# A transformer chain on one Trainium2 core: shared probability sums in the sequence attention, and three reorderings before it

## Time and profile before

| what | value |
|---|---|
| median of three runs | 1550.69 us (1550.03 to 1552.88) |
| profiled execution, its own time | 1555.64 us |
| its span, first to last instruction | 1553.9 us |
| busy share of the span | PE 90%, DVE 52%, ACT 47%, POOL 31% |
| granted TensorE clock, mean | 0.955 of full speed |

### The profile page before, as it was taken

One profiled execution on the slowest core, in us unless ns is written; L12 is line 12 of the kernel. 1 busy time (PEld: TensorE's weight loads), 2 busy tenths in 40 slices (PEclk: granted clock), 3 DMA queues, 4 the chain that ended last, 5 costly groups with the idle time before them and its releaser, 6 DMA issues. The chain is left out here.

```text
span 1553.9 us, 22502 instructions
## 1 busy us (share of the span) xinstructions
PE 1392.8 (90%) x8434; PEld 668.3 (43%) x8434; DVE 807.5 (52%) x1312; ACT 728.9 (47%) x1364; POOL 483.9 (31%) x522
## 2 busy tenths in 40 slices
PE   5678888788877989997899999989999999999998
PEld 4355655555533545552222222234444444444443
DVE  8864675566655778756666666525513211321220
ACT  3266666666665777772555565553501211210210
POOL 7211110356667676773222322144600000000000
PEclk9689999989989999997899999999999999999999
DMA  6646564746442001112644444233502002001000
GB/s 174 142 154 159 128 160 143 176 96 157 125 130 82 28 28 35 49 64 87 182 126 124 123 138 113 85 100 104 162 1 82 1 1 81 0 0 54 0 1 27
DMA packets 89447, 140.68 MB, mean 91 GB/s; under 512 B 8409, under 2 KB 47897, under 8 KB 88801
## 3 DMA queue, kind: packets, MB, share of 16 engines
q1 hardware_dynamic: 76544, 114.16, 27.0%
q10 hardware_dynamic: 12800, 25.17, 5.1%
HBM read 105.85 MB, written 33.46 MB: 90 GB/s over the span
## 5 line engine op out<-in xcount | busy, mean ns | idle before, releaser
L1792 DVE TENSOR_REDUCE c_negmax<-c_psA 128x1 f32<-128x512 f32 x256 | 165.9, 682 | 93.2 <-PE c_psA L1867 89.0
L2078 ACT ACTIVATE d_silu<-d_psGU 128x512 f32<-128x512 f32 x64 | 38.2, 596 | 344.7 <-PE d_psGU L2145 344.6
L2145 PE MATMUL d_psGU<-d_zt_hi,d_w_hi 128*128 128x512 bf16 x512 | 194.6, 380 | 4.0 <-ACT d_silu L2078 2.6
L2145 PE MATMUL d_psGU<-d_zt_lo,d_w_hi 128*128 128x512 bf16 x512 | 194.8, 381 | 0.0
L2145 PE MATMUL d_psGU<-d_zt_hi,d_w_lo 128*128 128x512 bf16 x512 | 194.8, 380 | 0.0
L1747 ACT ACTIVATE c_probs<-c_psB 128x512 f32<-128x512 f32 x256 | 140.4, 595 | 103.3 <-PE c_psB L1880 103.3
L894 DVE TENSOR_REDUCE a_negmax<-a_psX 128x4 f32<-128x1024 f32 x128 | 151.4, 1216 | 27.1 <-PE a_psX L1163 26.6
L2108 DVE TENSOR_TENSOR d_h<-d_psGU,d_silu 128x512 f32<-128x512 f32 x64 | 44.2, 691 | 223.7 <-PE d_psGU L2145 223.3
L753 ACT ACTIVATE a_probs<-a_psB 128x512 f32<-128x512 f32 x256 | 138.0, 592 | 18.8 <-PE a_psB L1175 18.2
L1867 PE MATMUL c_psA<-c_ks,c_qs 96*128 96x512 bf16 x256 | 104.0, 409 | 17.7 <-DVE c_negmax L1792 8.3
L1175 PE MATMUL a_psB<-a_qs,a_ks 115*128 115x256 bf16 x512 | 88.6, 292 | 33.4 <-ACT a_probs L753 31.4
(11 more groups left out here) (231 smaller groups left out, 2560.7 us busy)
## 6 DMA issues: line engine op xcount, KB each, us to landing
a_tern_stage<-in_w ACTq DMA_DIRECT2D x32, 768.0 KB, 5.8
d_weight_stage<-in_w_last SPq DMA_DIRECT2D x24, 512.0 KB, 4.2
a_ks<-k_scr SPq DMA_DIRECT2D x8, 768.0 KB
a_qs<-q_scr SPq DMA_DIRECT2D x8, 768.0 KB
c_ks<-k_scr SPq DMA_DIRECT2D x48, 128.0 KB, 2.6
c_qs<-q_scr SPq DMA_DIRECT2D x48, 128.0 KB, 3.0
a_xz<-in_x SPq DMA_DIRECT2D x32, 128.0 KB, 3.0
a_ctx<-in_ctx_t SPq DMA_DIRECT2D x8, 512.0 KB, 4.8
```

Of the source, the lines that this page charges most:

```text
L1792: v.tensor_reduce(negm[:, u:u + 1], A[:, u % 2, :], AX.X, ALU.max, negate=True)\
L2145: last = pe.matmul(GU[:, 2 * up + i % 2, :], wgu[wh][:, i, up, k, :], zt[zh][:, k, :], start=(k == 0 and j == 0), stop=(k == DC - 1 and j ...
```

## The change

In the masked attention all thirds of a group now come before `results`, and so does the normalisation of batch b+3 (at g == 6); the split of thirds over groups is new; the two logarithms of the weight scale come before the thirds; in the last batch the preparation of the FFN's first four tiles is dealt out in 12 parts over six groups.

In the ternary FFN `update(t - 3)` goes ahead of `gate(t, 1)` on DVE, one `take` moves up, and PE transposes x for tile t+1 ahead of `down(t - 2, 0)`.

In the sequence attention the exponentials have four buffers. For each quad, DVE adds key tile 0 and 1 of each head and POOL adds tile 2 and 3 (`added`, 128x512 f32 from SBUF to SBUF, four instructions each), and PE's `sums` then runs on each of the two added tiles: two groups of four matmuls for a quad in place of four. DVE's adds stand one by one between the maxima; the last quad keeps single sums for tiles 2 and 3. The end of a quad is spread over more time: `results` one step later, `turn_sums` at step 2 of the next quad, `turn_recips` and `finish` at the start of the quad after that.

```
-    THIRDS = (0, 2, 4, 1, 2, 1, 2, 0)
+    THIRDS = (0, 3, 3, 2, 1, 2, 1, 0)
...
-                    if g > 1:
-                        for k in behind[:1]:
-                            third(*k)
                     if to < BATCH:
                         exponentials(to, e + 1)
...
+                    for k in behind:
+                        third(*k)
+                    if g == 6 and b + 3 < BATCH:
+                        normalise(b + 3)
                     results(b, g)
...
-                    for k in behind[1 if g > 1 else 0:]:
-                        third(*k)
...
+                if t >= 3:
+                    update(t - 3)
                 if now:
                     gate(t, 1)
-                if t >= 3:
-                    update(t - 3)
...
-                    down(t - 3, n + 2) if n < 2 else down(t - 2, n - 2)
                     if n == 2:
                         for j in range(2):
                             transposed("x", t + 1, j)
+                    down(t - 3, n + 2) if n < 2 else down(t - 2, n - 2)
...
-        pr = sb("c_probs", [P, 2, 4, D], F32)
+        pr = sb("c_probs", [P, 4, 4, D], F32)
+        pairs = sb("c_prob_pairs", [P, 2, 4, D], F32)
...
+        def added(engine, unit, quads, pair, done, heads):
+            engine.wait_ge(s["exp_done"], MQ * quads + 8 * (pair + 1))
+            need(engine, s["sums_done"], 2 * quads + pair - 1)
+            for j in heads:
+                unit.tensor_tensor(pairs[:, pair, j, :], pr[:, 2 * pair, j, :], pr[:, 2 * pair + 1, j, :], ALU.add)\
+                    .then_inc(done, 1)
```

POOL's order for a batch, which replaces `spread(b - 1, 1)`, `context_low`, `low`, `update(b - 1, 1)`, `spread(b, 0)`, `update(b, 0)`:

```
             def attend(b, par, n, m):
+                k = 2 * b
+                if k >= 2:
+                    update(k - 2)
                 if m is not None:
                     front.normalised(pool, m)
+                if k:
+                    spread(k - 1)
                 if m is not None:
                     front.context_low(pool, m)
...
+                added(pool, g, k, 1, s["pair_pool"], range(4))
+                if m is not None:
+                    front.low(pool, m)
+                if k:
+                    update(k - 1)
+                spread(k)
+                if k + 1 < LAST:
+                    added(pool, g, k + 1, 1, s["pair_pool"], range(4))
```

The exponentials on ACT:

```
                     if j == 0:
-                        need(act, s["pv_done"], EG * b + e - 1)
+                        need(act, s["pv_done"], EG * b + e - 3)
+                        if e % 2 == 0:
+                            need(act, s["pair_pool" if e % 4 else "pair_dve"], (EG * b + e) // 4 * 4)
```

DVE, for k = 0..3 of a quad, after the maxima 4k and 4k + 1 and, in the last line, after 4k + 2 and 4k + 3:

```
+                        if q >= 2 and k == 0:
+                            finish(q - 2)
+                        if q and k == 2:
+                            reciprocals(q - 1)
+                        if k in (1, 2):
+                            added(dve, v, q, 0, s["pair_dve"], (2 * k - 2,))
...
+                        if k in (1, 2):
+                            added(dve, v, q, 0, s["pair_dve"], (2 * k - 1,))
```

The sums on PE, and their places (i = e % 4, turn 5 of a step):

```
+            def sums(k, pair):
+                if pair:
+                    pe.wait_ge(s["pair_pool"], 4 * (k + 1))
+                else:
+                    need(pe, s["ret_done"], k - 1)
+                    pe.wait_ge(s["pair_dve"], 4 * (k + 1))
+                for j in range(4):
+                    last = pe.matmul(OS[32 * j:32 * j + 32, k % 2, 1, :], keep["ones"][:, 0:32], pairs[:, pair, j, :],
+                                     start=(pair == 0), stop=(pair == 1))
...
-                            sums(b, e)
+                            if i == 0 and q:
+                                sums(q - 1, 1)
+                            if i == 3:
+                                sums(q, 0)
+                            if q == LAST and i == 3:
+                                last_sums(e - 1)
+                                last_sums(e)
```

More of the change, by code:

```diff
@@ L908, in split_max, with ahead @@
                 v.tensor_tensor(m2[:, half, 1], fixm[:, own], m2[:, half, 0], ALU.subtract).then_inc(s["m_split"], 1)
+            def ahead():
+                for t in range(front.EARLY):
+                    yield from front.prepare(dve, t)
             def attend(b):
@@ L1772, in attend @@
                         exponentials(b, e)
-                    if e == QT:
+                    if e == 1 and not begins(b):
+                        results(b - 1, 1)
+                    if e == QT + 1:
                         results(b, 0)
@@ L1825, in attend @@
                 for quad in range(2):
-                    last = (b, 0) if quad else (b - 1, 1)
-                    ends = quad == 1 or not begins(b)
+                    q = 2 * b + quad
                     if begins(b) and quad == 0:
@@ L1852, in _ @@
             run(dve, first, attend)
[L1853 to L1854 removed]
+            finish(LAST - 1)
+            reciprocals(LAST)
+            finish(LAST)
         @block.tensor
@@ L1889, in outputs @@
                     o = (4 * (e // QT) + j) * HD1
-                    pe.matmul(OS[32 * j:32 * j + 32, e // QT, 0, :], vt[par][:, kt, o:o + HD1], pr[:, e % 2, j, :],
-                              start=(kt == 0), stop=(kt == QT - 1))
-            def sums(b, e):
-                kt = e % QT
-                if kt == 0:
-                    need(pe, s["ret_done"], 2 * b + e // QT - 1)
-                for j in range(4):
-                    last = pe.matmul(OS[32 * j:32 * j + 32, e // QT, 1, :], keep["ones"][:, 0:32], pr[:, e % 2, j, :],
+                    last = pe.matmul(OS[32 * j:32 * j + 32, e // QT, 0, :], vt[par][:, kt, o:o + HD1], pr[:, e % 4, j, :],
@@ L1905, in turn_sums, with last_sums @@
+            def last_sums(e):
+                for j in range(4):
+                    last = pe.matmul(OS[32 * j:32 * j + 32, 1, 1, :], keep["ones"][:, 0:32], pr[:, e % 4, j, :],
+                                     start=False, stop=(e == EG - 1))
+                if e == EG - 1:
+                    last.then_inc(s["sums_done"], 1)
+            def turn_sums(k):
+                pe.wait_ge(s["os_copied"], k + 1)
                 for a in range(QT):
-                    last = pe.transpose(OS[:, quad, 1, a * P:(a + 1) * P], os_sb[:, quad, 1, a * P:(a + 1) * P], keep["ident"][:])
+                    last = pe.transpose(OS[:, k % 2, 1, a * P:(a + 1) * P], os_sb[:, k % 2, 1, a * P:(a + 1) * P], keep["ident"][:])
@@ L1928, in attend @@
                     quad, i = e // QT, e % QT
-                    last = (b, 0) if quad else (b - 1, 1)
-                    if i == 1 and (quad or not begins(b)):
-                        turn_sums(*last)
-                    if i == 3 and (quad or not begins(b)):
-                        turn_recips(*last)
+                    q = 2 * b + quad
+                    if i == 0 and q >= 2:
+                        turn_recips(q - 2)
+                    if i == 2 and q:
+                        turn_sums(q - 1)
                     steps = [1 if i > 0 or turn > 2 else 0 for turn in range(6)]
```

76 lines of the change are left out of this document (33 added, 43 removed).

## The result

The changed kernel takes 1538.62 us (median of four runs, 1535.73 to 1540.24), the kernel before 1551.79 on the same chip (1550.03 to 1554.32): a ratio of 0.9912, 95% interval 0.989 to 0.9934. Faster was right, but by 13 us where 28 were forecast. The profiled execution took 1537.69 us, its span 1535.9. The profiled execution of the kernel before had been a long one of its kind (1555.64 us, 3.9 above the median here), so the two profiles lie 18.0 us apart where the medians lie 13.2.

The account below looks back on a forecast made before the run. Each stage was taken as PE's own work plus the places where PE stands still. Terms of -23, -12 and +7 us gave -28 on 1555.6, so 1527.6, or 1523 for the median of 1550.69; range 1500 to 1545.

Parts of the forecast that it names:

- Stage one, -23: Masked attention: thirds and normalisation ahead of results give back 25 of 31.4 us of PE's waits, less 2 for DMAs.
- the sum: The prediction's addition over the three changed stages: -23 - 12 + 7 = -28 us.
- Stage two, -12: Ternary FFN: update ahead of the gate removes PE's stall at the down product, 1.06 us a tile over some 12 tiles.
- The safety bound: Ternary FFN: if rounded is not early enough for the x transposes, the stall moves there and 5 us is left.
- Stage three, +7: Sequence attention: DVE's additions and waits for POOL outweigh PE's saved sums, +1.7 us a batch in batches 1 to 5.
- The rival of the clock: Sequence attention: PE's clock falls to 1.2 GHz, +21 us a batch; 1586 us with three batches; chance 0.10.
- The lock: Sequence attention: DVE instructions with two SBUF inputs and POOL instructions reading SBUF exclude each other; waits of 0.7 and 1.5 us.
- The walk: Sequence attention, step-by-step estimate of a quad: odd 17.6 us, even 20.2, a batch 37.8 for 36.11.
- Stage one stays: Rival, masked attention: DVE's maxima and the thirds' DMAs bind at once, -8 for -23, 1538 us; chance 0.20.
- No exclusion: Rival, sequence attention: DVE's additions don't wait for POOL, -5 us for the stage in place of +7, 1511 us; chance 0.14.
- additions hidden: Rival, sequence attention: DVE's additions are hidden and PE's time comes back, some 25 us, 1491 us; chance 0.12.
- The range: Whole kernel: 1500 to 1545 us, the upper end for stage one staying and 5 us of stage two lost.

Follow-up runs that it names:

- The split of edits: Stages one and two changed, sequence attention as before, with only update moved (1521.85 us) or only PE's transposes moved (1526.48 us) in stage two; one profiled run each.
- the early scales: Stages one and two changed, sequence attention as before, plus POOL's chain of x scales one link group earlier: 1517.84 us, ratio 0.9777 against the kernel before.
- the spread scales: Stages one and two changed, sequence attention as before, with POOL's x-scale links spread over two tiles: 1508.99 us, ratio 0.9735 against the kernel before.

## Why the prediction was right and wrong

By the medians of the kernels with one stage's edits each, stage one gave -22.6 us, stage two -3.8 (-7.6 to -0.8) and stage three +14.9 (+9.9 to +19.1), against -23, -12 and +7. So two terms failed, by some 8 us each, and both the same way.

- **Stage one, -23: right in size, and only in part for its reasons.** PE's waits on a_probs went to 0.5 us where "under 10" was asked, which is 31 us. The new waits for DVE's maxima took 7.2 of them back (the sum has 6 for that) and those for the late copies 4.5 (the sum has 2), so waits alone give 19. The rest came from where the prediction had nothing: PE's own busy time, 8 us shorter for the same products in the pair of profiles, with less time at the lower clock. That the fewer stalls raised the clock fits, but no run shows it by itself. Normalisation is 7.5 us of the stage, forecast 7.2.
- **Stage two, -12: the step that failed.** It read "The stall goes: (1.91 + 0.21) / 2 = 1.06 us a tile, over some 12 tiles", and of the x transposes "need `rounded`, which is done about as early". `rounded` was not early. kx arrives late on POOL, and ACT already waited for it. PE's stall was slack of a longer ring (DVE's gates, POOL's gated, POOL's chains, ACT's rounding): it went, and 1.58 us a pair appeared at two other places, so that the period fell by 0.2 us and not by 2.1. The safety bound under it, "5 us is left", took the stall to move to one place only. The split of edits, the early scales (under half back) and the spread scales (all back and 0.3 us a pair more, 15.0 us less in the stage than with the two edits alone) show the ring, and both its links.
- **Stage three, +7: right in mechanism, mis-sized.** It measured +14.9 alone by the medians, and +10.5 and +10.9 in two traces. The undisturbed quads came as walked: 20.33 and 17.44 us for 20.2 and 17.6, a batch of 37.77 for 37.8, additions of 0.68 us with one of 2.00 in the even quad. By the marks of `high` on ACT, in the profiles, batch 0 gave -1.6 (forecast -2.5), the next four steady batches +0.8, +1.6, +1.7 and +1.6, the fifth +4.2, and the rest +2.6 (forecast +1.1). What the sum had at nothing is the clock: 2.4 of the 4.2 us lie in two even quads at a fallen clock. The slower executions of this stage's kernel had lower mean clocks, which goes the same way; how much of the +14.9 is the clock was not measured. The rival of the clock had priced it as a whole batch at 1.2 GHz, 21 us. In the changed kernel a fall costs an even quad 1.0 or 1.4 us, and the clock is back at 1.00 within two stretches of 5 us.
- **The lock** was priced right for the additions. The walk left out `split_max`, whose subtraction is held by POOL too (1.20 and 2.06 us for 0.17), and so is its cast with one SBUF input (0.88). The subtraction stands in front of PE's transpose.
- **The rivals.** "Stage one stays" landed on the measured time, 1538, by the wrong road: stage one gained all, stage two almost nothing. "No exclusion" and "additions hidden" are refuted by the same rows.
- **The range** held, and with some luck: it reached to 1545 for a stage one that gains little and a stage two that loses 5 us. Neither is what happened: the errors lay in stage two, by another mechanism, and in stage three.

## What to carry to other kernels

A stall that recurs with a period is worth what it shows only if nothing else in that period runs in a ring of the same length. Before counting it, take each wait in the period and ask what that wait would be if the stall were gone. Here the one to ask about was ACT's 1.6 us for kx, on an engine that was not the bound, just ahead of what PE needs next; with the stall gone it became 3.05.

DVE instructions with two SBUF inputs (and the small cast here) and long ones on POOL should be laid out as if they shared one queue, the smallest ones included: a 0.17 us subtraction beside a 2.13 us one took 2.06 us, and where PE's next instruction hangs on it, PE pays.

## What was not expected of the hardware

- The smaller the DVE instruction, the larger the hold in proportion: 128x16, two SBUF inputs, 0.17 us with POOL quiet and 1.19 to 2.06 beside POOL's instructions of 1.27 and 2.13 us. A cast of 128x16 from f32 to bf16, with one SBUF input, was held as well, 0.88 us beside an addition of POOL and up to 1.54 beside a subtraction of 2.13.
- It works both ways. A 128x2 `tensor_scalar` of POOL took 1.08 us in stage two, beside DVE's 2.24 us product of two SBUF inputs, where others of the same shape take 0.23 or 0.24.
- In the changed kernel, PE busy for 3.20 of 5 us was followed by a stretch at a granted clock of 0.66 in one quad, and by none below 1.00 in another in which PE, DVE and ACT were busy for the same time to a hundredth of a microsecond.
